# Statistics of the first layer moved into the gather that precedes it, and its end cut into four groups of tiles

## The reference

```python
h = bn(x @ w1.T + b1, g1, beta1)                  # statistics over all nodes
agg = segment_sum(h[src], dst)
h = gelu(agg @ wr.T + br + h @ wroot.T)
out = bn(h @ w2.T + b2, g2, beta2) + x
x = layernorm(x + out)                            # end of layer 0
support = x @ W                                   # layer 1 begins
x = layernorm(x + segment_sum(support[src] * w, dst) + b)
```

## Time and profile before

| | us |
|---|---|
| median of 3 runs | 8134.57 (8119.32 to 8135.34) |
| the profiled execution, its own time | 8166.52 |
| its span, first to last instruction | 8164.4 |
| end of the first gather stage to the first scatter of layer 1 | 1243.5 to 1643.7 |

### The profile page before, as it was taken

One profiled execution on the slowest core, in us unless ns is written; L12 is line 12 of the kernel. 1 busy time (PEld: TensorE's weight loads), 2 busy tenths in 40 slices (PEclk: granted clock), 3 DMA queues, 4 the chain that ended last, 5 costly groups with the idle time before them and its releaser, 6 DMA issues.

```text
span 8164.4 us, 63474 instructions
## 1 busy us (share of the span) xinstructions
PE 4404.2 (54%) x16396; PEld 3297.9 (40%) x16396; DVE 2658.4 (33%) x5923; ACT 871.3 (11%) x2038; POOL 5203.9 (64%) x4804
## 2 busy tenths in 40 slices
PE   3445458876666661444445445445454445555557
PEld 2233338754545540233334333334333334433336
DVE  5332112565555554111112111112111114444445
ACT  0000002233232220000001000001000001000002
POOL 4766660078888883666663666664666663677774
PEclk9776679988888885677777676677676777766768
DMA  2333324066666665333332333333233333666662
GB/s 63 90 92 92 92 84 134 4 70 72 71 72 72 72 71 172 89 92 92 93 92 84 90 91 92 92 92 94 87 92 92 92 91 99 179 181 182 182 183 65
DMA packets 490414, 804.29 MB, mean 99 GB/s; under 512 B 96624, under 2 KB 360344, under 8 KB 490072
## 3 DMA queue, kind: packets, MB, share of 16 engines
q0 software_dynamic: 300288, 615.29, 33.1%
q1 hardware_dynamic: 189784, 184.91, 7.1%
HBM read 645.97 MB, written 153.86 MB: 98 GB/s over the span
## 4 chain that ended last, share of the span: by engine, by line
another core or an unknown queue 31%; PE 25%; POOL 18%; issue 15%; DVE 7%; DMA 2%; DVEq 1%; SPq 0%; ACT 0%; POOLq 0%; ACTq 0%
PE acc L576 18%; POOL sums_by_src L456 11%; POOL ring L434 8%; DVE onehot L1074 3%; PE acc L495 2%; PE acc L500 2%; DMA sums_by_src<-ring,E 1%; DVE X L1103 1%; DVEq L1073 1%; PE high L495 1%; PE high L500 1%; PE high L486 1%; DMA ring<-table_x,idx_dst 0%; DVE stats L1100 0%
## 5 line engine op out<-in xcount | busy, mean ns | idle before, releaser
L576 PE MATMUL acc<-ring,onehot 128*128 x8320 | 2764.4, 495 | 3100.4 <-DVE onehot L1074 2073.3
L576 PEld LDWEIGHTS acc<-ring,onehot 128*128 128x128 f32 x8320 | 1993.8, 249 | 3868.4 <-issue 3510.3
L434 POOL DMA_INDIRECT ring<-table_g,idx_dst x2346 | 2290.7, 976 | 1350.0 <-issue 683.5
L1074 DVE TENSOR_TENSOR onehot<-iota_row,dl_dst 128x512 f32<-128x512 f32 x1040 | 719.9, 693 | 3904.1 <-remote 2563.2
L456 POOL DMA_INDIRECT sums_by_src<-ring,E x782 | 1208.2, 1545 | 677.8 <-ACT high L876 439.6
L434 POOL DMA_INDIRECT ring<-table_x,idx_dst x782 | 836.4, 1070 | 428.4 <-issue 347.7
L434 POOL DMA_INDIRECT ring<-in_x_dram,idx_dst x782 | 793.0, 1014 | 407.2 <-issue 243.7
L718 PE MATMUL high<-H,ring 128*128 x1664 | 542.6, 483 | 457.4 <-ACT high L876 445.5
L718 PEld LDWEIGHTS high<-H,ring 128*128 128x128 f32 x1664 | 374.0, 236 | 552.2 <-issue 492.7
L820 ACT COPY H<-acc 128x256 f32<-128x256 f32 x196 | 72.9, 372 | 4487.8 <-PE acc L576 2744.3
L1288 DVE TENSOR_SCALAR ring<-acc,E 128x128 f32<-128x128 f32 x832 | 283.9, 403 | 572.5 <-PE acc L504 572.5
(11 more groups left out here) (250 smaller groups left out, 2809.8 us busy)
## 6 DMA issues: line engine op xcount, KB each, us to landing
E<-in_edge_attr_dram SPq DMA_DIRECT2D x781, 128.0 KB
ring<-table_g,idx_dst POOLq DMA_INDIRECT x2346
sums_by_src<-ring SPq DMA_DIRECT2D x3, 6272.0 KB, 39.2
table_g<-H SPq DMA_DIRECT2D x147, 128.0 KB, 1.7
ring<-sums_by_src SPq DMA_DIRECT2D x36, 512.0 KB, 4.5
ring<-in_x_dram,idx_dst POOLq DMA_INDIRECT x782
sums_by_src<-ring,E POOLq DMA_INDIRECT x782, 3.8
ring<-table_x,idx_dst POOLq DMA_INDIRECT x782
```

Source lines behind the costliest of these rows:

```text
L434: pool.indirect_dma_start(out=ring_v[:, b % SLOTS, 0:D], out_offset=None, in_=table[name][:, :], in_offset=bass.IndirectOffsetOnAxis(ap=id ...
L576: pe.matmul(acc4[:, ds(to, width)], onehot[:, (q * BATCH + j) % ONEHOTS, :], ring[:, ds(slot, width)], start=False, stop=True, skip_group_ ...
L1074: last = tt(onehot[:, s:s + BATCH, :], iota_row[:, :].unsqueeze(1).to_broadcast((P, BATCH, P)), dl_ap[which][:, q * BATCH:(q + 1) * BATCH] ...
```

## The change

Part one moves the statistics pass into the first gather stage. At steps q = 40, 42, ... 136 PE's `between` transposes one x tile, DVE's `first_pass` copies it (in ACT's place), PE multiplies it by w1 one step later, and DVE takes the statistics two steps after that. SP loads each tile inside `relay`, ten groups ahead, into seven buffers that are idle then (rows of `bias`, `wt["b"]`, `wt["d"]`); w1 comes early and is turned at step 36. After the stage x is still loaded into XR. The convolution now transposes XR beside X, and ACT copies it to H there.

Part two cuts the end of the layer into groups of 13 tiles (`ZG`; 13, 13, 13, 10): statistics and `layer_norm` by group, with each group's `normal` laid between the next group's three steps. PE lays the remaining products between the tiles of layer 1's table; a group's root stands in ACT's loop over that table, and the root of the degrees behind the loop. The bias is no longer added to X: it is the first value of one of the three sums.

```diff
@@ SP
+                    t = y_step(k, -10) if n == 0 else None
+                    if t is not None:
+                        if t >= YB:
+                            sp.wait_ge(sm("y_turned"), t - YB + 1)
+                        elif t == 3 + DH:
+                            sp.wait_ge(sm("w_turned"), 1)
+                        if t >= 3:
+                            sp.wait_ge(sm(f"x_in{t % 3}"), 16 * (t // 3))
+                        rows_ = min(P, N - t * P)
+                        load(y_rows_in[t % YB][0:rows_, :], a["x"][t * P:t * P + rows_, :], sm(f"x_in{t % 3}"))
...
+                first_value = bias[:, 1, :] if j == 0 else zero
                 sp.dma_start(sums[j][0:NP, :].rearrange("(p t) d -> p t d", t=T),
-                             zero.unsqueeze(1).to_broadcast((P, T, D))).then_inc(sm("sums_in0"), 16)
+                             first_value.unsqueeze(1).to_broadcast((P, T, D))).then_inc(sm("sums_in0"), 16)
@@ PE
+            def between(q):
+                rows_of_pairs(q)
...
+                t = y_step(q, 0)
+                if t is not None:
+                    pe.wait_ge(sm(f"x_in{t % 3}"), 16 * (t // 3 + 1))
...
+                        pe.wait_ge(sm("y_xT"), t - 1)
+                    turn(bank[4 + t % 2], y_rows_in[t % YB]).then_inc(sm("y_turned"), 1)
+                t = y_step(q, 1)
+                if t is not None:
...
+                    pe.wait_ge(sm("y_xT"), t + 1)
+                    if t >= 2:
+                        pe.wait_ge(sm("y_stats"), t - 1)
+                    to_features(bank[6 + t % 2], [(wt["a"], y_turned_in[t % 2])]).then_inc(sm("y_mm"), 1)
+            sum_pairs(0, between)
-            for i in range(T + 1):
-                if i < T:
...
-                    turn(bank[i % 2], tile(XR, i)).then_inc(sm("y_turned"), 1)
...
-                    to_features(bank[2 + t % 2], [(wt["a"], tile(H, t))]).then_inc(sm("y_mm"), 1)
...
                     turn(bank[i % 2], tile(X, i)).then_inc(sm("conv_turned"), 1)
+                    turn(bank[i % 2][:, D:2 * D], tile(XR, i)).then_inc(sm("conv_turned"), 1)
...
+            for t in range(min(T, ZG + 2)):
+                z_product(t)
...
+                if i + ZG + 2 < T:
+                    z_product(i + ZG + 2)
@@ ACT
-            for t in range(T):
-                act.wait_ge(sm("y_turned"), t + 1)
-                sc.copy(tile(H, t), bank[t % 2][:, 0:D]).then_inc(sm("y_xT"), 1)
...
+                    sc.copy(tile(H, i), bank[i % 2][:, D:2 * D]).then_inc(sm("conv_xT"), 1)
...
-            root(std[:, :], rstd[:, :], 3)
-            root(dis[:, :], deg[:, :], 4)
...
+                    if i % ZG == 0:
+                        here = z_group(i // ZG)
+                        root(std[:, here[0]:here[-1] + 1], rstd[:, here[0]:here[-1] + 1], 3 + i // ZG)
...
+            root(dis[:, :], deg[:, :], 3 + NZ)
@@ DVE
+            def first_pass(q):
...
+                t = y_step(q, 0)
+                if t is not None:
+                    dve.wait_ge(sm("y_turned"), t + 1)
+                    if t >= 2:
+                        dve.wait_ge(sm("y_mm"), t - 1)
+                    copy(y_turned_in[t % 2], bank[4 + t % 2][:, 0:D]).then_inc(sm("y_xT"), 1)
+                t = y_step(q, 3)
+                if t is not None:
+                    dve.wait_ge(sm("y_mm"), t + 1)
+                    n = LAST if t == T - 1 else P
+                    for h in range(DH):
+                        last = nc.vector.bn_stats(stats[:, h, t * 6:(t + 1) * 6], bank[6 + t % 2][:, h * P:h * P + n])
+                    last.then_inc(sm("y_stats"), 1)
...
                 one_hots(0, q)
                 rows_of_edges(q)
+                first_pass(q)
...
+            for i in range(ZG + 2):
+                last = z_steps(z_group(0), i) or last
+            for g in range(NZ):
+                link(last)
+                layer_norm(3 + g, z_group(g))
+                for i in range(-2, ZG + 2):
+                    if 0 <= i + 2 < len(z_group(g)):
+                        t = g * ZG + i + 2
+                        normal(t, tile(X, t)).then_inc(sm("ln0_rows"), 1)
+                    last = z_steps(z_group(g + 1), i) or last
             link(ts(deg[:, :], deg[:, :], 1.0, None, ALU.add))
-            for t in range(T):
-                normal(t, tile(X, t)).then_inc(sm("ln0_rows"), 1)
-            ask_root(4)
+            ask_root(3 + NZ)
             link(nc.vector.reciprocal(dis[:, :], dis[:, :]))
-            dve.wait_ge(sm("b_in"), 16)
-            for t in range(T):
-                dve.wait_ge(sm("y1_turned"), t + 1)
-                tt(tile(X, t), tile(X, t), bias[:, 1, :], ALU.add).then_inc(sm("seed_rows"), 1)
```

More of the change, by code:

```diff
@@ L21 @@
 BEHIND = 4
+ZG = 13
+Y0 = 40
+YS = 2
 SUMS = 3
-XG = 13
+XG = 17
 BANKS = 4
@@ L176, in gnn_kernel, with y_step @@
         Z = ring[:, 20 * D:20 * D + 8 * D]
+        y_rows_in = [bias[:, i, :] for i in range(3)] + [wt[w_][:, i, :] for w_ in "bd" for i in range(DH)]
+        YB = len(y_rows_in)
+        y_turned_in = [wt["c"][:, i, :] for i in range(DH)]
+        def y_step(q, lag):
+            t, r = divmod(q - Y0 - lag, YS)
+            return t if r == 0 and 0 <= t < T else None
+        assert Y0 + YS * T + 4 < 160
         block = ctx.enter_context(nc.Block())
@@ L893, in _ @@
                 clear_rows(g)
-            root(std[:, :], rstd[:, :], 5)
+            root(std[:, :], rstd[:, :], 4 + NZ)
             act.wait_ge(sm("ln1_own"), T)
@@ L922, in _ @@
             gcn(2)
-            root(std[:, :], rstd[:, :], 8)
+            root(std[:, :], rstd[:, :], 7 + NZ)
             act.wait_ge(sm("ln2_rows"), T)
@@ L1085, in messages, with layer_norm @@
                 ts(g, g, 0.0, None, ALU.max).then_inc(sm("landed5"), here)
[L1087 to L1095, removed]
+            def layer_norm(n, tiles=range(T)):
+                cut = slice(tiles[0], tiles[-1] + 1)
+                st = ln_stats.rearrange("p (t c) -> p t c", c=6)[:, cut, :]
+                mean_, rstd_, w0, w1, w2 = mean[:, cut], rstd[:, cut], ln_w[:, 0, cut], ln_w[:, 1, cut], ln_w[:, 2, cut]
+                tt(mean_, st[:, :, 1], st[:, :, 4], ALU.add)
+                tt(w0, st[:, :, 1], st[:, :, 4], ALU.subtract)
+                link(tt(w1, st[:, :, 2], st[:, :, 5], ALU.add))
+                ts(mean_, mean_, 0.5, None, ALU.mult)
+                link(stt(w2, w0, 0.25, w0, ALU.mult, ALU.mult))
+                link(stt(rstd_, w1, 1.0 / D, w2, ALU.mult, ALU.add))
+                link(ts(rstd_, rstd_, EPS, None, ALU.add))
                 ask_root(n)
-                link(nc.vector.reciprocal(rstd[:, :], std[:, :]))
+                link(nc.vector.reciprocal(rstd_, std[:, cut]))
             def row_stats(t, v):
@@ L1244, in _ @@
             dve.sem_inc(sm("z_weights"), 1)
[L1245 to L1256, removed]
@@ L1257, in _, with z_rows, z_shift, z_stats @@
-            link(last)
-            layer_norm(3)
+            def z_rows(t):
+                dve.wait_ge(sm("z_product"), t + 1)
+                stt(tile(X, t), tile(XR, t), 2.0, bank[t % 2][:, 0:D], ALU.mult, ALU.add).then_inc(sm("z_v"), 1)
+            def z_shift(t):
+                dve.wait_ge(sm("z_v"), t + 1)
+                tt(tile(X, t), tile(X, t), bias[:, 2, :], ALU.add).then_inc(sm("z_shifted"), 1)
+            def z_stats(t):
+                dve.wait_ge(sm("z_shifted"), t + 1)
+                return row_stats(t, tile(X, t))
@@ new lines, in z_steps @@
+            def z_steps(tiles, i):
+                last = None
+                if 0 <= i < len(tiles):
+                    z_rows(tiles[i])
+                if 0 <= i - 1 < len(tiles):
+                    z_shift(tiles[i - 1])
+                if 0 <= i - 2 < len(tiles):
+                    last = z_stats(tiles[i - 2])
+                return last
+            for i in range(ZG + 2):
[8 more added lines that the diff above has]
+                    last = z_steps(z_group(g + 1), i) or last
```

66 lines of the change are left out of this document (37 added, 29 removed).

## The result

The changed kernel takes 8076.5 us (median of 4, 8076.18 to 8077.78) against 8128.0 us of the kernel before in the same series (8119.32 to 8135.34): a ratio of 0.9939, 95% interval 0.9927 to 0.9951, 51.5 us less. 8081 was forecast, in a range of 8048 to 8125. In a second series both kernels were slower, 8104.2 and 8161.3, with a ratio of 0.9923 (0.9909 to 0.9936), 57.2 us less.

What follows compares the result with a forecast made beforehand. Taken as bound: gathers in the gather stages, then 400 us in which one engine after another works alone. Terms −58 + 11 − 15 + 0 + 8 = −54 took 8134.57 to 8081 us; range 8048 to 8125.

Steps and rivals of the forecast that it cites:

- The statistics pass: Between the first gather stage's end and the first batch norm's root: the root comes 60.8 us earlier.
- The stage's cost: First gather stage with the pass in it: +8 us, twice the larger difference between stages; bounds −4 and +151.
- POOL's own speed: Gathers beside the new DVE work in the first stage: 0 us, as added instructions read PSUM with one input.
- The convolution: From first root to first product with the last weights: +14 us; the convolution itself 177 us, not 166.
- The transposes' term: Convolution: one transposed pair more for each tile, 49 × 0.22 = +11 us.
- the cold start: Convolution pays for PE's start at 1.2 GHz, from which the pass had warmed it before: some 3 us.
- The groups: Product, layer norm and table interleaved, PE the bound at 1.96 us a tile: first product to first spread −15 us.
- The border term: The three later layer norms, PE's remaining 5.0 us against DVE's about 5: 0 to 2 us each, 3 in all.
- The clock: PE's low clock after idling about 5 us in the first layer norm: taken as 2 us lost.
- The hidden edits: Bias as a first value drops 49 DVE adds that lay in the table's shadow: 0 us.
- Rival B: PE falls to the low clock in the groups, its 83 us doubling: 8164 us, slower; chance 0.04.
- The signs: Expected marks: first stage's window 1036 to 1050 us, waits below 110, root after 13 us, convolution 177, groups 109.

Runs made afterwards that it cites:

- recorded pair: First single traces of the kernel before and the changed kernel, not of one series; spans up to the first scatter differ by −65.2 us.
- control: The kernel before once more, no edit: 8163.1 us, ratio 0.9998 to the kernel before.
- part two: Kernel before with only the layer's end in four groups and the bias row as first value, statistics pass left behind the stage: 8153.7 us, ratio 0.9989.
- the bias row alone: Kernel before with only the bias row as one sum's first value, its 49 adds dropped: 8165.5 us, ratio 0.9996.
- again: The changed kernel once more, no edit: 8104.2 us, ratio 0.9923 to the kernel before.
- part one: Kernel before with only the statistics pass inside the first gather stage and the convolution transposing x itself: 8119.6 us, ratio 0.9936.
- tripled one: Changed kernel with w1 products and statistics added to the first gather stage made three times: 8073.2 us, ratio 0.9938 to the kernel before.

## Why the prediction was right, step by step

**The statistics pass.** The step from the stage's end to the root was forecast at −60.8 and measured at −61.4 and −58.1, by the mechanism given: weight copies, table load, root.

**The stage's cost.** +8 was taken, between −4 and +151. It measured −6 in the recorded pair, which is no pair of one series, and +13.5 in the second. In the two series at 8161 and 8169 the stage ends at 1239.7 to 1240.3 without the pass (control, part two, the bias row alone) and at 1248.0 to 1253.8 with it (again, part one, the two kernels with groups of seven): +10 on the mean of three and four traces. In the later series at 8128 it ends at 1242.3 to 1245.4 with the pass, and at 1248.8 with the tripled one; no trace without it was taken there. So the term was right within a few us, by luck in its size: it was taken as twice a difference between two stages, and no mechanism gave it. Of the 10 some 6.5 us lie between the 65th issue and the last take (1037.7 to 1038.4 us without, 1042.4 to 1045.2 with, in those two series), where the waits for freed slots go from 93 to 96 us to 102 to 106; of the rest 2 lie ahead of the 65th issue and 2 behind the last gather's start. That last part, the draining, is anything from 34 to 43 us, with the pass and without it, and the recorded pair's −6 lies in it alone (39.7 to 33.8). That three times the work costs only 3 to 7 us more is shown; what sets the cost's size is not.

POOL's own speed held (731.9 to 731.5 us for 718 gathers). The 1.44 us of a gather beside a one-hot is no typical one: counted over the stage in the trace of before, 112 gathers that overlap a one-hot and nothing else on DVE took 0.94 to 1.44 us, 1.03 on the mean. In the changed kernel the 18 that overlap an added copy or statistic alone took 0.94 to 0.95.

**The convolution.** +14 forecast, +9.7 and +11.1 measured. The transposes' term held: its first product comes 15.3 us behind the root, 15.9 before, and the rest grows by 10.3, which is 49 × 0.21. The other 3 us, the cold start, did not appear: the chain ahead of the convolution was granted 0.63, as before 0.64, and the window from 1263 on 1.00. The warmth of the pass had been lost in that chain before the change too, by a row that the prediction itself quotes.

**The groups.** −15 forecast, −9.7 and −12.3 measured. The bound, PE, was right, and the sum of 1.96 us a tile stands in the trace (1.95 from copy to copy). Two terms of its sum were mis-sized, the border and the clock.

The border term was taken at "0 to 2 us each, 3 in all". The step that failed is the comparison of PE's remaining 5.0 us of work with DVE's chain of about 5: it has no term for ACT's queue, where the root has to wait for a copy, and the copy for a product on PE. PE's pauses at the three borders were 1.84, 1.84 and 1.28 us in both traces of the changed kernel, 5.0 in all; moving the root took them to 0.4, 0.4 and none.

The clock was put down with 2 us, behind the first layer norm alone. Between the groups' roots lie 28.5 and 29.3 us in the recorded trace but 26.8 and 27.6 in the second one, with the same pauses. The difference is the granted clock; windows of the recorded trace, then of the second (columns as in the earlier trace rows), the whole stretch first and then 5 us behind the first layer norm and behind the first border:

```profile
1448.00:1563.00 115.00, 104.25 (x491) 85.73 (x492) 74.65 (x237) 34.81 (x107) 0.00 (x0) 0.95 0.01 4
1470.00:1475.00 5.00, 5.00 (x18) 3.96 (x17) 3.10 (x10) 0.90 (x3) 0.00 (x0) 0.69 0.00 0
1497.00:1502.00 5.00, 5.00 (x17) 4.05 (x18) 2.86 (x9) 0.65 (x2) 0.00 (x0) 0.66 0.00 0
```
```profile
1466.00:1578.00 112.00, 101.45 (x491) 83.86 (x492) 74.44 (x238) 34.98 (x107) 0.00 (x0) 0.98 0.01 4
1486.00:1491.00 5.00, 4.53 (x24) 3.76 (x23) 4.70 (x15) 1.39 (x4) 0.00 (x0) 1.00 0.00 0
1513.00:1518.00 5.00, 4.52 (x23) 3.96 (x24) 4.46 (x14) 1.54 (x5) 0.00 (x0) 1.00 0.00 0
```

By an estimate from these shares, (0.31 + 0.34) × 5 / 0.5 = 6.5 us ran at 1.2 GHz in the recorded trace, and half of it, 3.2 us, was lost; 114.5 and 111.5 differ by 3.0. Why the same pauses brought the clock down in one trace and not in the other stays open.

Behind the table the root of the degrees cost the 2.3 us of a first spread that waits for DVE, near the 2.46 put down for it (0.55 of it stood there before), and up to the first scatter some more (+2.3 and +0.7), which the forecast had at 0.

**The hidden edits.** The bias row: 0, measured alone. Rival B: with 0.95 and 0.98 granted over the stretch it did not arise at its price of 83 us, only in small, as 3 us in one trace of two. The 0.89 of the window from 1448 belongs to the batch norm ahead of it, granted 0.72 from 1438 to 1448.

**The sum.** −54 forecast; −65 and −45 by steps, −51.5 and −57.2 by medians. Steps and medians differ because the steps are single traces: the one of the kernel before ran 8166.5 us, 38 above the median of its runs, and the one of *again* 8110.9, 7 above. That the sum came so near is in part luck: the convolution took 3 to 4 us less than forecast, and the groups with what follows to the first scatter 3 to 8 more.

**The signs.** The window of the first stage stayed at 1037 to 1045 us with waits of 96 to 106 (1036 to 1050 and below 110 were named), its end moved by less than 30 us, PE waited for no DMA in the convolution, and the last copy of the table ended 12.8 us behind the layer norm's last step.

## What to carry to other kernels

When two stages are laid between each other, add up both stages' work on every engine before taking the slower chain's engine as the bound: the product that cost nothing under VectorE's 1.08 us became 0.87 of TensorE's 1.96. A pass moved into a stage that waits for gathers was nearly free here, about 10 us for some 60 saved; making its work three times as large is the way to see whether there is room left. That its hand-overs were laid several steps ahead is a likely reason, which no run tests. In an engine that serves two streams in a hand-written order, ask of each short step on the path which longer wait stands ahead of it in the queue: here the root's line, at two borders just one copy earlier, took away a pause of TensorE at each of three.

## What the runs showed that was not expected

The gather stages have a level of their own that goes with the series: the three stages behind the scatter that gather from `table_g` last 1106 to 1111 us from first to last gather in the later series at 8128, and 1112 to 1118 in the two at 8161 and 8169, there in kernels with and without the change alike; the last stage 1113 to 1132 and 1138 to 1144. The recorded trace of the kernel before has the lengths of the slower series (1113 to 1114, and 1141), that of the changed kernel those of the faster (1110 to 1111, and 1131). The chip alone doesn't set the level: the later series at 8128 and the one at 8169 ran on the same chip. What does is not shown. A recorded trace of one series must therefore not be subtracted from one of another: of the 90 us between the first two spans 25 lie behind the first scatter, 20 of them in these four stages.
